# Attention stage of a graph network: one-hots turned in pairs, tile numbers loaded in thirds, source one-hots two tiles ahead

## The chip, the cores and the metric

The kernel runs on one core of a Trainium2 chip. A core has five engines that each work through an instruction stream of their own: PE (matmul), DVE (VectorE), ACT (ScalarE), POOL (GpSimd) and SP, which here mostly starts transfers. They wait for each other by semaphores. The metric is the device time of one execution in microseconds (us).

## The reference, cut to what matters

Two layers of a graph network over 6250 nodes and 206250 edges, sorted by their target node `dst`. The change concerns the first layer, a graph attention with 4 heads of 32 features, which the kernel computes in its attention stage:

```python
h = (x @ W.T).reshape(N, H, OUT)              # x is normalised and clipped first
a_src = (h * att_src).sum(-1)
a_dst = (h * att_dst).sum(-1)
alpha = jax.nn.leaky_relu(a_src[src] + a_dst[dst], 0.2)
amax = jax.ops.segment_max(alpha, dst, num_segments=N)
ex = jnp.exp(alpha - amax[dst])
denom = jax.ops.segment_sum(ex, dst, num_segments=N)
msg = h[src] * (ex / denom[dst])[:, :, None]
out = jax.ops.segment_sum(msg, dst, num_segments=N)
```

The second layer (gathers of node rows, two matmuls for each edge, another sum over targets) follows in stages that the change does not touch.

## The kernel before

**Tiles and batches.** The edges form 1612 tiles of 128, one edge for each partition, and 62 batches (`NB`) of 26 tiles (`BT`). Since the edges are sorted, the targets of a tile lie in two neighbouring tiles of 128 nodes. Their number, the tile's bin, is kept in `bin_row` and is read into engine registers by `bins`: one load of 26 numbers at the start of each batch, on DVE for batch b and on PE for batch b + 2.

**What is done for a tile t of batch b.** POOL gathers the rows h[src] (line 494) into `G`. DVE's `hot` (line 935) writes a one-hot of the targets, 128 edges x 256 nodes in bf16, into `OHb`. PE's `turn` (line 1453) transposes it in two halves into a PSUM bank, one of two; ACT's `turn_out` (line 621) copies it to `ohT`, also two buffers. PE's `expand` (line 1463) multiplies it with the table `aT3` to give each edge the logits of its target. All this is done two batches ahead, for batch b + 2, while batch b is summed. From the logits of batch b + 1 a chain of small steps on DVE, PE and ACT (`chain`, spread over the tiles by `STEPS`) makes the segment maxima and the exponentials; its first step (line 954) also needs the gathered rows of batch b + 1.

For the batch b itself, ACT's `widen` (line 628) copies the one-hot as fp32 into one of four buffers `OH`. DVE's `product` (line 1022) makes the messages `msg`. PE's aggregation (line 1525) multiplies the widened one-hot with the messages into one of two PSUM banks, and DVE's `add_up` (line 1042) adds that bank to the node tile `acc` in SBUF.

**What sets the order.** Each engine's order is written out by hand in its `batch` function, a loop over t; nothing else schedules. In pass t before the change:

- DVE: hot(b+2, t), add_up(b, t-2), then products and a step of the chain.
- PE: turn(b+2, t), expand(b+2, t-1), aggregation(b, t), sometimes small matmuls of the chain.
- ACT: widen(b, t+2), turn_out(b+2, t), sometimes small copies of the chain.

**Who waits for whom.** An aggregation of tile t waits for `acc_done`, that is add_up(t-2) has emptied its bank. add_up(t) waits for `agg_ready` of tile t. widen(t) waits for `agg_ready` of tile t-4, since there are four buffers `OH`. hot(b+2, t) overwrites the slot of tile t in batch b and waits for `wide_ready` of that tile. turn(b+2, t) waits for `oh_ready` of tile t and for `ohT_ready` of tile t-2; turn_out(t) for `ohT_ps` of tile t and for `expanded` of tile t-2. POOL's gather for tile t of batch b+2, where t is odd, waits for `agg_ready` of tile t in batch b.

The first two batches are turned ahead of the loop. Batches 2 to 57 (on ACT to 59) run in hardware loops with two batches in a body, so that a jump comes with every second batch; batches 0, 1 and 58 to 61 are written out.

## Time and profile before

| | us |
|---|---|
| median of 3 runs | 5811.69 |
| lowest, highest run | 5804.10, 5815.06 |
| the profiled execution: time | 5807.29 |
| the profiled execution: span, first to last instruction | 5805.4 |
| attention stage in it | about 149 to 2257 |

| engine | busy us | share of the span |
|---|---|---|
| PE (matmul) | 5114.6 | 88% |
| DVE | 4028.8 | 69% |
| POOL | 3923.5 | 68% |
| ACT | 2891.4 | 50% |

Busy time is the time in which an engine works on an instruction; loads of registers, jumps and waits are not in it. The shares are means over stages that have different limits, so a stage is read by itself. In brackets behind an instruction stands how long its engine sat idle before it and what ended that; "issue" means that the engine waited for nothing that the profile shows.

### The profile page before, as it was taken

Reading aid. Unit: us, or ns where it says so; the run is one execution under the profiler, and the core shown is the slowest. Engines: PE = TensorE matmul, PEld = TensorE weight load, DVE = VectorE, ACT = ScalarE, POOL = GpSimd, SP = SyncE. Lnnn points to the kernel's source line nnn. Section 1 sums busy time; section 2 is a strip of 40 time slices with the busy share of each in tenths; the row PEclk is TensorE's granted clock in tenths of the full one; section 3 lists DMA queues with packets and bytes.
Section 4 is the critical chain, followed back from the end, with each engine's and each line's share of the span. In section 5 each row is a group of like instructions: output and inputs, shape, how many; then the busy total and the mean of one; then the engine's idle time right before and its main releaser. Section 6 shows DMA issues by size and latency. Waiting matters only on the chain.

```text
span 5805.4 us, 160391 instructions
## 1 busy us (share of the span) xinstructions
PE 5114.6 (88%) x34498; PEld 4012.9 (69%) x34499; DVE 4028.8 (69%) x14406; ACT 2891.4 (50%) x8241; POOL 3923.5 (68%) x3713
## 2 busy tenths in 40 slices
PE   4888888888888886899999999999987999999999
PEld 3677777776677775667666666666665777777777
DVE  6777777777777778555555555555555888888887
ACT  3555555555555553333333333333224777777776
POOL 4777777777777775677777777777776545555553
PEclk6898888888888887999999999999998999999999
DMA  4422222222222225899888899988896999999997
GB/s 108 161 54 52 52 53 53 52 53 53 53 52 52 53 62 165 261 262 269 261 263 260 255 262 260 257 261 253 256 256 182 214 214 211 213 216 215 213 214 187
DMA packets 860289, 993.31 MB, mean 171 GB/s; under 512 B 307992, under 2 KB 663224, under 8 KB 859774
## 3 DMA queue, kind: packets, MB, share of 16 engines
q1 hardware_dynamic: 662494, 608.23, 40.1%
q0 software_dynamic: 190592, 378.22, 24.3%
q10 hardware_dynamic: 6816, 3.38, 0.2%
q14 instruction: 349, 2.86, 0.2%
q8 instruction: 38, 0.62, 0.0%
HBM read 726.65 MB, written 262.76 MB: 170 GB/s over the span
## 4 chain that ended last, share of the span: by engine, by line
PE 55%; DMA 12%; DVE 10%; issue 10%; POOL 7%; DVEq 4%; ACT 2%; POOLq 0%; SPq 0%; ACTq 0%
PE bank L1525 12%; PE bank L1684 11%; PE bank L1617 7%; DMA xr<-arena 7%; PE bank L1619 7%; POOL xr L542 7%; PE bank L1674 6%; DMA arena<-p_tab,arena 3%; PE bank L1453 3%; DVE arena L1042 2%; DVEq L246 2%; DVE arena L935 2%; PE bank L1607 1%; DMA arena<-h_tab,arena 1%; PE bank L1665 1%
## 5 line engine op out<-in xcount | busy, mean ns | idle before, releaser
L494 POOL DMA_INDIRECT arena<-h_tab,arena x1612 | 1591.7, 987 | 582.9 <-issue 399.5
L542 POOL DMA_INDIRECT xr<-arena x1612 | 1587.3, 985 | 510.7 <-issue 350.3
L1525 PE MATMUL bank<-arena 128*128 128x136 f32 x6448 | 1299.7, 329 | 96.6 <-DVE arena L1042 8.1
L703 ACT ACTIVATE arena<-bank 128x256 f32<-128x256 f32 x1612 | 595.9, 385 | 1405.6 <-PE bank L1619 1050.2
L556 POOL DMA_INDIRECT arena<-p_tab,arena x428 | 668.4, 1562 | 658.7 <-DMA arena<-p_tab,arena 443.4
L1525 PEld LDWEIGHTS bank<-arena 128*128 128x128 f32 x6448 | 966.3, 211 | 201.8 <-issue 109.0
L621 ACT ACTIVATE arena<-bank 128x256 bf16<-128x256 bf16 x1612 | 618.2, 384 | 888.9 <-PE bank L1453 833.6
L1617 PE MATMUL bank<-arena 128*128 128x256 f32 x3224 | 1010.3, 395 | 42.4 <-DVE arena L1236 25.2
L1619 PE MATMUL bank<-arena 128*128 128x256 f32 x3224 | 972.5, 383 | 28.6 <-DVE arena L1252 25.5
L1684 PE MATMUL bank<-arena 128*128 128x257 f32 x3424 | 898.8, 385 | 3.8 <-ACT arena L780 3.2
L1042 DVE TENSOR_TENSOR arena<-arena,bank 128x272 f32 x1612 | 692.2, 429 | 181.5 <-PE bank L1525 163.7
L1619 PEld LDWEIGHTS bank<-arena 128*128 128x128 f32 x3224 | 605.4, 190 | 148.6 <-DVE arena L1252 69.9
L628 ACT ACTIVATE arena<-arena 128x256 f32<-128x256 bf16 x1612 | 645.1, 408 | 89.7 <-issue 66.7
L1684 PEld LDWEIGHTS bank<-arena 128*128 128x128 f32 x3424 | 586.2, 191 | 75.2 <-issue 5.0
L1617 PEld LDWEIGHTS bank<-arena 128*128 128x128 f32 x3224 | 537.6, 198 | 135.8 <-issue 49.4
L935 DVE TENSOR_SCALAR arena<-arena 128x256 bf16<-128x256 bf16 x1612 | 461.0, 289 | 219.5 <-issue 210.3
L1453 PE MATMUL bank<-arena 128*128 128x128 bf16 x3224 | 489.0, 238 | 136.6 <-DVE arena L935 134.5
L1252 DVE COPY arena<-bank 128x128 f32<-128x128 f32 x806 | 233.2, 289 | 512.4 <-PE bank L1607 512.2
L780 ACT ACTIVATE arena<-arena 128x512 f32<-128x512 f32 x856 | 535.6, 626 | 98.7 <-DVE arena L1347 74.9
L1674 PE MATMUL bank<-arena 128*128 x3852 | 566.8, 274 | 1.9 <-DVE arena L1347 1.0
L1236 DVE TENSOR_SCALAR arena<-arena 128x128 f32<-128x128 bf16 x1612 | 474.1, 306 | 79.9 <-PE bank L1619 46.6
L1347 DVE TENSOR_TENSOR arena<-arena,bank 128x512 f32<-128x512 f32 x856 | 469.0, 548 | 1.8 <-PE bank L1674 1.8
(253 smaller groups left out, 6596.8 us busy)
## 6 DMA issues: line engine op xcount, KB each, us to landing
arena<-xr SPq DMA_DIRECT2D x428, 516.0 KB, 3.9
arena<-q_tab SPq DMA_DIRECT2D x1612, 128.0 KB
arena<-in_edge_attr SPq DMA_DIRECT2D x61, 832.0 KB
arena<-rel_tab SPq DMA_DIRECT2D x124, 224.0 KB
arena<-h_tab,arena POOLq DMA_INDIRECT x1612
xr<-arena POOLq DMA_INDIRECT x1612
arena<-rel_tab SPq DMA_DIRECT2D x124, 192.0 KB
xr<-arena SPq DMA_DIRECT2D x26, 516.0 KB
```

The source lines that it names most:

```text
L494: pool.indirect_dma_start(G[:, q, t, :], None, h_tab, bass.IndirectOffsetOnAxis(ap=idx[:, q, t:t + 1], axis=0)).then_inc(sem(f"gath{q}"), 16)
L542: pool.indirect_dma_start(xr, bass.IndirectOffsetOnAxis(ap=pos[:, q, t:t + 1], axis=0), Rb[:, t, :], None).then_inc(sem(f"scat{m}"), 16)
L556: pool.indirect_dma_start(XR[:, s, k, RW:RW + HID], None, p_tab, bass.IndirectOffsetOnAxis(ap=sidx[:, s, k:k + 1], axis=0), compute_op=ALU ...
L621: A.activation(ohT[:, t % 2, :], PSB[t % 2][:].bitcast(BF16)[:, 0:2 * P], ACT.Copy).then_inc(sem("ohT_ready"), 1)
L628: A.activation(OH[:, (t + 2 * q) % 4, :], OHb[:, q, t, :], ACT.Copy).then_inc(sem("wide_ready"), 1)
L1042: V.tensor_tensor(a, a, PSB[3 + t % 2][:, 0:2 * H * MW], ALU.add).then_inc(sem("acc_done"), 1)
L1453: last = pe.transpose(PSB[t % 2][:].bitcast(BF16)[:, k * P:(k + 1) * P], OHb[:, s, t, k * P:(k + 1) * P], identb)
L1525: last = pe.matmul(PSB[3 + t % 2][:, k * H * MW:(k + 1) * H * MW], OH[:, (t + 2 * q) % 4, k * P:(k + 1) * P], flat(msg[:, t, :, :]), start ...
L1617: pe.matmul(o, OHT[:, (t + 2 * q) % 4, :], Qw[:, t, :], start=True, stop=False)
L1619: pe.matmul(o, EAT[:, (t // 2 + q) % 2, :], w1z[:, t % 2, :], start=False, stop=True).then_inc(sem("main_done"), 1)
L1674: last = pe.matmul(PSB[2 + m % 2][:, j * HID:(j + 1) * HID], ohTp[:, m % 2, j, :], flat(Pt[:, bass.ds(reg, 1), part, :]), start=(part == 0 ...
L1684: last = pe.matmul(PSB[4 + m % 2][:, 0:XW], OHp[:, m, j, :], hid[:, m % 2, j, :], start=(j == 0), stop=(j == PR - 1))
```

## The change

In the batches of the attention stage:

- `turn` and `turn_out` work on a pair g of tiles (2g and 2g+1): four transposes into one PSUM bank, one copy of 512 columns, every second pass. `ohT` has room for two pairs.
- `expand` runs two tiles behind, in pass t for tile t-2; the last two tiles of a batch are expanded in passes 0 and 1 of the next, for which PE reads their two numbers again.
- `hot` runs two tiles ahead: pass t makes tile t+2 of batch b+2, and tiles 0 and 1 of batch b+3 are made at the end of batch b, among the last two add_ups.
- The tile numbers are loaded in three parts of 8 or 9, on DVE in passes 0, 8 and 17, on PE in passes 1, 9 and 18.
- The second half of the logits' sum on DVE moves from pass 1 to pass 3.

The diff, cut to its core:

```diff
         S = Region(Z0)
-        aRes, ohT, OH, msg = S([NT + 1, 2 * H]), S([2, 2 * P], BF16), S([4, 2 * P]), S([BT, H, MW])
+        aRes, ohT, OH, msg = S([NT + 1, 2 * H]), S([2, 2, 2 * P], BF16), S([4, 2 * P]), S([BT, H, MW])
         abS, vE, isl4 = S([2, BT, 2 * H]), S([H, BT]), S([H, BT])
...
             return v.rearrange(f"p {d} -> p ({d})") if len(v.shape) > 2 else v
+        NG2 = BT // 2
+        LOADS = [(k * BT // 3, (k + 1) * BT // 3) for k in range(3)]
         PIECES = [(m * BT // 4, (m + 1) * BT // 4) for m in range(4)]
...
         block = ctx.enter_context(nc.Block())
-        def bins(engine, b, count):
+        def bins(engine, b, lo, count):
             return nc.values_load_multi_w_load_instructions(
-                bin_row[0:1, bass.ds(b * RB, count)], engines=[engine], min_val=0, max_val=NT - 1,
+                bin_row[0:1, bass.ds(b * RB + lo, count)], engines=[engine], min_val=0, max_val=NT - 1,
                 skip_runtime_bounds_check_because="a node's tile, clamped at 0")[1]
...
                     projected(k - 2)
-            def turn_out(b, t, first=False):
-
-                act.wait_ge(sem("ohT_ps"), b * BT + t + 1)
-                if not (first and t < 2):
-                    act.wait_ge(sem("expanded"), b * BT + t - 1)
-                A.activation(ohT[:, t % 2, :], PSB[t % 2][:].bitcast(BF16)[:, 0:2 * P], ACT.Copy).then_inc(sem("ohT_ready"), 1)
+            def turn_out(b, s, g, first=False):
+
+                act.wait_ge(sem("ohT_ps"), b * NG2 + g + 1)
+                if not (first and g < 2):
+                    act.wait_ge(sem("expanded"), b * BT + 2 * g - 2)
+                k = (s * NG2 + g) % 2
+                A.activation(flat(ohT[:, k, :, :]), PSB[k][:].bitcast(BF16)[:, 0:4 * P], ACT.Copy).then_inc(sem("ohT_ready"), 1)
             def widen(b, q, t, first=False):
...
             act.wait_ge(sem("cols_used"), 2)
-            for t in range(BT):
-                turn_out(0, t, True)
+            for g in range(NG2):
+                turn_out(0, 0, g, True)
             act.wait_ge(sem("rb_init"), 2)
...
             chain_exp(0, True)
-            for t in range(BT):
-                turn_out(1, t)
+            for g in range(NG2):
+                turn_out(1, 1, g)
             def batch(b, q, ahead2=True, ahead1=True, first=False):
...
                         widen(b, q, t + 2, first)
-                    if ahead2:
-                        turn_out(b + 2, t)
+                    if ahead2 and t % 2 == 0:
+                        turn_out(b + 2, q, t // 2)
                     if ahead1 and t == 1:
...
                 b, n = 2 * i + q, 2 * i + q + 1
-                regs = bins(ENG.DVE, b, BT)
+                regs = []
                 for t in range(BT):
-                    if ahead2:
-                        hot(b + 2, q, t)
+                    if ahead2 and t + 2 < BT:
+                        hot(b + 2, q, t + 2)
+                    for lo, hi in LOADS:
+                        if t == lo:
+                            regs += bins(ENG.DVE, b, lo, hi - lo)
                     if t == 0:
...
                         V.tensor_tensor(a, a, fac.unsqueeze(2).to_broadcast([P, H, MW]), ALU.mult).then_inc(sem("acc_done"), 1)
-                        if ahead1:
-                            logits(b + 1, 1 - q, 1)
                     if t >= 2:
                         add_up(b, t - 2, regs)
+                    if ahead1 and t == 3:
+                        logits(b + 1, 1 - q, 1)
                     if t in (3, 7):
...
                         product(1 - q, 1, 3)
-                add_up(b, BT - 2, regs)
-                add_up(b, BT - 1, regs)
+                for t in range(2):
+                    if ahead3:
+                        hot(b + 3, 1 - q, t)
+                    add_up(b, BT - 2 + t, regs)
                 if table == "runs":
...
             logits(1, 1, 0)
+            for t in range(2):
+                hot(2, 0, t)
             batch(0, 0)
...
                 last.then_inc(sem("counted"), 1)
-            def turn(b, s, t, first=False):
-                pe.wait_ge(sem("oh_ready"), b * BT + t + 1)
-                if not (first and t < 2):
-                    pe.wait_ge(sem("ohT_ready"), b * BT + t - 1)
-                for k in range(2):
-                    last = pe.transpose(PSB[t % 2][:].bitcast(BF16)[:, k * P:(k + 1) * P], OHb[:, s, t, k * P:(k + 1) * P], identb)
+            def turn(b, s, g, first=False):
+                u = (s * NG2 + g) % 2
+                pe.wait_ge(sem("oh_ready"), b * BT + 2 * g + 2)
+                if not (first and g < 2):
+                    pe.wait_ge(sem("ohT_ready"), b * NG2 + g - 1)
+                for t in range(2):
+                    for k in range(2):
+                        last = pe.transpose(PSB[u][:].bitcast(BF16)[:, (2 * t + k) * P:(2 * t + k + 1) * P], OHb[:, s, 2 * g + t, k * P:(k + 1) * P], identb)
                 last.then_inc(sem("ohT_ps"), 1)
-            def expand(b, t, regs, first=False):
-
-                pe.wait_ge(sem("ohT_ready"), b * BT + t + 1)
+            def expand(b, s, t, reg, first=False):
+
+                g = t // 2
+                if t % 2 == 0:
+                    pe.wait_ge(sem("ohT_ready"), b * NG2 + g + 1)
                 half, j = divmod(t, BT // 2)
...
                 for k in range(2):
-                    last = pe.matmul(ab_ps[half][:, j, :, :].rearrange("p s c -> p (s c)"), ohT[:, t % 2, k * P:(k + 1) * P],
-                                     flat(aT3[:, bass.ds(regs[t] + k, 1), :, :]), start=(k == 0), stop=(k == 1))
+                    last = pe.matmul(ab_ps[half][:, j, :, :].rearrange("p s c -> p (s c)"), ohT[:, (s * NG2 + g) % 2, t % 2, k * P:(k + 1) * P],
+                                     flat(aT3[:, bass.ds(reg + k, 1), :, :]), start=(k == 0), stop=(k == 1))
                 last.then_inc(sem("expanded"), 1)
...
             pe.wait_ge(sem("hx_used"), NCH)
-            regs = bins(ENG.PE, 0, BT)
-            for t in range(BT):
-                turn(0, 0, t, True)
-                if t:
-                    expand(0, t - 1, regs, True)
-            expand(0, BT - 1, regs, True)
+            regs = bins(ENG.PE, 0, 0, BT)
+            for g in range(NG2):
+                turn(0, 0, g, True)
+                for t in range(max(2 * g - 2, 0), 2 * g):
+                    expand(0, 0, t, regs[t], True)
+            for t in range(BT - 2, BT):
+                expand(0, 0, t, regs[t], True)
             chain_resets(0)
...
             chain_carry(0)
-            regs = bins(ENG.PE, 1, BT)
-            for t in range(BT):
-                turn(1, 1, t)
-                if t:
-                    expand(1, t - 1, regs)
-            expand(1, BT - 1, regs)
+            regs = bins(ENG.PE, 1, 0, BT - 2)
+            for g in range(NG2):
+                turn(1, 1, g)
+                for t in range(max(2 * g - 2, 0), 2 * g):
+                    expand(1, 1, t, regs[t])
             def batch(b, q, ahead2=True, ahead1=True, first=False, table=""):
-                if ahead2:
-                    regs = bins(ENG.PE, b + 2, BT)
+                regs, late = [], bins(ENG.PE, b + 1, BT - 2, 2) if ahead1 else []
                 pe.wait_ge(sem("g_ready"), b + 1)
...
                 for t in range(BT):
+                    if ahead2 and t % 2 == 0:
+                        turn(b + 2, q, t // 2)
+                    if t < 2 and ahead1:
+                        expand(b + 1, 1 - q, BT - 2 + t, late[t])
                     if ahead2:
-                        turn(b + 2, q, t)
-                        if t:
-                            expand(b + 2, t - 1, regs)
+                        for lo, hi in LOADS:
+                            if t == lo + 1:
+                                regs += bins(ENG.PE, b + 2, lo, hi - lo)
+                        if t >= 2:
+                            expand(b + 2, q, t - 2, regs[t - 2])
                     pe.wait_ge(sem("wide_ready"), b * BT + t + 1)
...
                                 step(b + 1)
-                if ahead2:
-                    expand(b + 2, BT - 1, regs)
             batch(0, 0, first=True)
...
```

Where instructions stand now. First ACT, around passes 2 and 3 of a batch in the loop; the 256-column copy from a PSUM bank is `turn_out`, the 128x256 copy within `arena` (the SBUF) is `widen`, the copies 1x4x26 to 1x4 are the chain's resets. Before:

```order
L627 REGISTER_ALU [waits agg_ready]
L628 ACTIVATE arena<-arena 128x256 [waits oh_ready]
L618 REGISTER_ALU
L621 ACTIVATE arena<-bank 128x256 [waits expanded,ohT_ps]
```

After:

```order
L620 REGISTER_ALU
L624 ACTIVATE arena<-bank 128x512 [waits expanded,ohT_ps]
L639 ISA [waits cin_ready]
L639 ACTIVATE arena<-arena 1x4x26
L640 ISA
L640 ACTIVATE arena<-arena 1x4x25
L641 ACTIVATE arena<-arena 1x4
L630 REGISTER_ALU [waits agg_ready]
L631 ACTIVATE arena<-arena 128x256 [waits oh_ready]
```

Before, each widen was followed by one copy from PSUM; now one copy of twice the width stands ahead of two widens.

Next PE, passes 4 and 5 of a batch in the loop: `turn` (128x128), `expand` (128x24), aggregation (128x136), and a transpose of the chain (104x128). Before, for one pass:

```order
L1449 REGISTER_ALU
L1453 MATMUL bank<-arena 128x128 [waits ohT_ready,oh_ready]
L1453 MATMUL bank<-arena 128x128
L1463 ISA [waits ohT_ready]
L1463 MATMUL bank<-arena 128x24
L1463 ISA
L1463 MATMUL bank<-arena 128x24
L1518 REGISTER_ALU
L1521 REGISTER_ALU [waits msg_ready,wide_ready]
L1525 MATMUL bank<-arena 128x136 [waits acc_done]
L1525 MATMUL bank<-arena 128x136
```

After, for the even pass (the odd one has no turn and its `expand` no wait):

```order
L1460 REGISTER_ALU
L1465 MATMUL bank<-arena 128x128 [waits ohT_ready,oh_ready]
L1465 MATMUL bank<-arena 128x128 x3
L1472 REGISTER_ALU
L1477 ISA [waits ohT_ready]
L1477 MATMUL bank<-arena 128x24
L1477 ISA
L1477 MATMUL bank<-arena 128x24
L1537 REGISTER_ALU
L1540 REGISTER_ALU [waits msg_ready,wide_ready]
L1544 MATMUL bank<-arena 128x136 [waits acc_done]
L1544 MATMUL bank<-arena 128x136
```

All four transposes of a pair stand behind the aggregation of the odd tile before it.

Last DVE, at the first instructions of the loop's body: `hot` is the TENSOR_SCALAR 128x256, the tile numbers the TENSOR_LOAD. Before:

```order
L1147 ISA
L246 TENSOR_LOAD arena
L934 ISA
L935 ISA [waits wide_ready]
L935 TENSOR_SCALAR arena<-arena 128x256
L1052 REGISTER_ALU
L1053 TENSOR_SCALAR arena<-bank 128x4 [waits fac_ps]
```

After:

```order
L1157 ISA
L938 ISA [waits wide_ready]
L938 TENSOR_SCALAR arena<-arena 128x256
L248 ISA
L248 TENSOR_LOAD arena
L1058 REGISTER_ALU
L1059 TENSOR_SCALAR arena<-bank 128x4 [waits fac_ps]
```

The load is now behind the first `hot` and is a third as long; the `hot` is that of tile 2.

## Rows read from the trace of the kernel before

**Rows 1.** Windows, attention stage: length, busy time (instructions) by engine, PEclk, DMA share, GB/s.

```profile
149.00:2257.00 2108.00, 1736.97 (x14171) 1483.63 (x14171) 1658.67 (x6311) 1164.01 (x3599) 1534.80 (x1569) 0.88 0.26 65
```

**Rows 2.** Groups by line, 500 to 1800 us: busy us, mean ns, idle before.

```profile
L494 POOL DMA_INDIRECT arena<-h_tab,arena x986 | 967.6, 981 | 333.6 <-issue 242.1 <-PE bank L1525 91.5
...
L628 ACT ACTIVATE arena<-arena 128x256 f32<-128x256 bf16 x984 | 393.5, 407 | 45.2 <-issue 45.1
L621 ACT ACTIVATE arena<-bank 128x256 bf16<-128x256 bf16 x983 | 377.1, 384 | 535.4 <-PE bank L1453 500.9 <-PE bank L1463 14.9 <-issue 12.5
```

**Rows 3.** Waits, 500 to 1800 us: total us, times, longest.

```profile
POOL arena L494 <- PE bank L1525: 91.5, 235, 2.7
...
DVE arena L954 <- DMA arena<-h_tab,arena: 24.2, 19, 1.9
```

**Rows 4.** Timeline around two starts of a batch: start, duration, [idle before <-releaser].

```profile
1037.36 0.95 POOL L494 DMA_INDIRECT arena<-h_tab,arena  x1 [0.30 <-issue]
1037.99 1.03 ACT L628 ACTIVATE arena<-arena 128x256 f32<-128x256 bf16 x3 [2.48 <-issue]
...
1041.69 0.43 DVE L935 TENSOR_SCALAR arena<-arena 128x256 bf16<-128x256 bf16 x1 [4.92 <-issue]
...
1073.60 0.29 DVE L935 TENSOR_SCALAR arena<-arena 128x256 bf16<-128x256 bf16 x1 [1.99 <-issue]
```

**Rows 5.** Timeline, one tile at full clock, same columns.

```profile
1048.40 0.43 DVE L1042 TENSOR_TENSOR arena<-arena,bank 128x272 f32 x1
...
1049.11 0.53 PEld L1525 LDWEIGHTS bank<-arena 128*128 128x128 f32 x4 [0.21 <-DVE arena L1042]
...
1050.00 0.72 PE L1525 MATMUL bank<-arena 128*128 128x136 f32 x4
...
1050.45 0.21 PEld L1453 LDWEIGHTS bank<-arena 128*128 128x128 bf16 x2
...
1050.56 0.28 PE L1453 MATMUL bank<-arena 128*128 128x128 bf16 x2
...
1050.87 0.38 ACT L621 ACTIVATE arena<-bank 128x256 bf16<-128x256 bf16 x1 [0.20 <-PE bank L1453]
...
1051.15 0.41 ACT L628 ACTIVATE arena<-arena 128x256 f32<-128x256 bf16 x1
1051.33 0.26 DVE L935 TENSOR_SCALAR arena<-arena 128x256 bf16<-128x256 bf16 x1
...
1051.51 0.43 DVE L1042 TENSOR_TENSOR arena<-arena,bank 128x272 f32 x1
```

**Rows 6.** Timeline, batches 59 and 60: who waits for ACT, ACT for PE.

```profile
2135.79 1.03 ACT L628 ACTIVATE arena<-arena 128x256 f32<-128x256 bf16 x3 [2.67 <-issue]
2136.28 0.29 DVE L935 TENSOR_SCALAR arena<-arena 128x256 bf16<-128x256 bf16 x1 [1.89 <-ACT arena L628]
...
2220.85 0.42 ACT L628 ACTIVATE arena<-arena 128x256 f32<-128x256 bf16 x1 [0.56 <-PE bank L1525]
```

**Rows 7.** Source lines, tile-number loads, 26 (L246) and 12 (L252): ns min/median/max.

```profile
L246 DVEq TENSOR_LOAD <-arena x62: 2060/2070/4694, 141.5 to 2233.8; - x62
...
L252 DVEq TENSOR_LOAD <-arena x108: 845/852/1094, 4439.0 to 5760.0; - x108
```

**Rows 8.** Source line, an ACT copy of 512 columns in a later stage.

```profile
L780 ACT ACTIVATE arena<-arena x65: 618/625/634, 4599.7 to 4698.7; 128x512 f32<-128x512 f32 x65
```

**Rows 9.** Windows, after a start, in mid-batch, in a last batch.

```profile
1042.00:1048.00 6.00, 5.75 (x36) 5.43 (x36) 4.47 (x18) 3.54 (x13) 3.79 (x5) 0.53 0.21 48
1049.00:1070.00 21.00, 19.61 (x180) 16.58 (x180) 20.26 (x81) 13.40 (x41) 15.36 (x16) 1.00 0.21 47
2216.00:2233.00 17.00, 14.90 (x98) 11.63 (x97) 15.51 (x57) 8.61 (x22) 0.00 (x0) 0.93 0.41 107
```

**Rows 10.** Timeline, PE's weight loads at half clock.

```profile
1043.85 0.96 PEld L1525 LDWEIGHTS bank<-arena 128*128 128x128 f32 x4
...
1044.70 0.38 PEld L1453 LDWEIGHTS bank<-arena 128*128 128x128 bf16 x2
```

## The prediction

> **What bounds the kernel now.** I read the stages first. The attention stage runs from about 149 to 2257 us; every other stage issues the same instructions in both kernels. Over it PE, DVE and POOL are all 73% to 82% busy, so no share names the bound [rows 1]. The groups by line say more: 986 gathers (L494) keep POOL for 967.6 us with 333.6 us idle ahead of them, one every 1.32 us, so a batch of 26 takes 34.3 us [rows 2]. An unhindered gather takes 0.95 us with 0.30 us ahead of it [rows 4], 1.25 in all, 32.6 us for a batch. POOL is therefore nearly the bound, and in every second batch DVE waits for gathered rows [rows 3]. PE and DVE are close behind: DVE stands idle for 2.0 us where a batch starts inside the loop body and for 4.9 us where the loop closes, every second batch [rows 4].
>
> The last view is one tile at full clock [rows 5]. PE's aggregation of tile t (L1525) needs add_up(t - 2) on DVE (L1042); one aggregation starts 0.89 us after the other (1049.11 and 1050.00). ACT's two copies are only used a tile or more later, so nothing waits for them. That slack is what the change spends.
>
> **The change part by part.** *Removed.* The 26 tile numbers are one load of 2.07 us on DVE [rows 7], and PE's is alike. It explains the stall of 2.0 us inside the body, and 2.07 of the 4.9 us at the loop's end; the other 2.8 us is the jump. 12 numbers take 0.85 us [rows 7], so one costs (2.07 - 0.85) / 14 = 0.087 us and a third, 8 or 9 numbers, an estimated 0.6 to 0.75 us. The bounds are nothing, where the engine waits anyway, and 0.85, the load of 12. The Trainium skill ("DMA: Bandwidth & Descriptors", Latency and other measured facts) gives such a load a floor of about 600 ns. No row here has fewer than 12 numbers to show it; by it PE's new load of two numbers would cost 0.6 instead of 0.17 us, some 25 us more over 60 batches.
>
> *Turned in pairs.* PE turns two one-hots in a row, and ACT copies 512 columns instead of twice 256. The copy of 256 holds ACT for 0.28 us, from 1050.87 to 1051.15 [rows 5]. A further 256 columns cost 0.625 - 0.408 = 0.22 us by ACT's other copies [rows 2, 8], or 0.28 if all is doubled. The pair holds ACT for 0.50 to 0.56 us; I take 0.53. [...]
>
> *One-hots two tiles ahead.* This part decides. On DVE hot(b+2, t+2) now stands ahead of add_up(t - 2), and it waits for wide_ready of tile t + 2: ACT must first have widened the old one-hot of that slot. widen(t + 2) in turn waits until aggregation t - 2 has freed one of four buffers. Before, DVE asked here for widen(t), which needed aggregation t - 4. Two tiles of slack are gone. Queued behind that wait on DVE is add_up(t - 2), and for that PE's aggregation t waits. ACT's order makes it worse: for even t it runs widen(t + 2), the paired copy, widen(t + 3), and the copy waits for PE's turn, which PE issues behind aggregation t - 1. So there is a ring: aggregation t - 1, turn, paired copy, widen(t + 3), hot(t + 3), add_up(t - 1), aggregation t + 1. Its steps at full clock:
> - from the aggregation's start to the turn behind it, 1050.00 to 1050.56: 0.56 us [rows 5]
> - the turn until ACT starts, 1050.56 to 1050.87: 0.31, and 0.21 for two more transposes by their weight loads: 0.52 [rows 5]
> - the paired copy, until widen can start: 0.53
> - widen 0.41, and 0.07 to the hot that waited for it (the first of three widens that start at 2135.79 ends at 2136.20; hot starts at 2136.28): 0.48 [rows 2, 6]
> - from hot to add_up's start, 1051.33 to 1051.51: 0.18 [rows 5]
> - from add_up's start to the aggregation that waited for it, 1048.40 to 1049.11: 0.71 [rows 5].
>
> That is 2.98 us for two tiles, above the 1.8 they take in these rows and above the 2.5 that two gathers take. Bounds: 2.88 with the copy at 0.50 and no hand-over; 3.22 with the copy at twice 0.384. At half clock the aggregation's weights take 0.96 instead of 0.53 us and a turn's 0.38 instead of 0.21 [rows 10], so the ring takes 0.43 + 0.34 more, some 3.8. That a widen can wait for an aggregation and start at its end is seen in the last batches, where ACT has nothing else to do [rows 6].
>
> *The sum for a batch.* The ring binds from tile 1 to tile 23, 11 turns: 32.8 us. Once in each batch there also lie on it: ACT's three small copies and DVE's logits around tiles 2 to 4, about 0.7; PE's small matmuls behind aggregation 7, which wait for the backward scan and so start late, about 0.9; the one behind aggregation 11, 0.5; and the load on DVE at tile 17, between hot and add_up, 0.7. That makes 2.8, an estimate whose parts are sums of operations of 0.2 to 0.4 us; its bounds are 1.4 and 4. The loads on DVE at tiles 0 and 8 fall where it waits over 1 us for ACT, and PE's ahead of aggregations that wait for add_up: nothing there, 0.7 each without that cover. Tiles 23 to 25 take twice 0.9 to 1, as now: 1.9. From tile 25 to tile 1 of the next batch PE issues a small matmul, the first pair, two late expansions, an aggregation and its load, about 3.3. Inside the body a batch takes 32.8 + 2.8 + 1.9 + 3.3 = 40.8 us.
>
> At the loop's end hot(b+3, 0) on DVE waits for widen(b+1, 0), which ACT does only after its own jump of 2.5 us [rows 4]; the last add_ups and DVE's jump of 2.8 come behind that. The two jumps lay side by side, now one follows the other: about 4 us above a start inside the body, 44.8. Both batches: 85.6. After each start PE's clock is low for some us (0.53 from 1042 to 1048, full from 1049) [rows 9]; one ring and a third at 3.8 instead of 2.98 adds 1.1 a batch: 87.8.
>
> Against 2 x 34.3 = 68.6 now that is 19.2 us more for two batches. 60 of the 62 batches turn one-hots ahead: 30 x 19.2 = 576 us. The two batches turned before the loop get some 3 us quicker (0 to 6). The profiled execution took 5807.29 us, 1.9 above its span and 4.4 under the median of the runs, 5811.69. 5807 + 576 - 3 = 6380, and halfway to the median's basis **6383 us**.
>
> **The rivals.** *A: the gathers stay the bound, and it gets faster.* If the ring closes in less than the 2.5 us of two gathers, only the gain at the starts counts. PE holds POOL up for 91.5 us in 235 cases [rows 3], of which 235 x 0.30 = 70.5 is POOL's usual gap: 21 us in 37.9 batches, 0.55 each, and 60 of them vanish: -33, and -2 at the tail: 5772. For it speaks that DVE already waits for gathered rows in every second batch, so that POOL needs only a little more speed elsewhere; against it, that the ring would have to lose 0.5 us, one whole step.
>
> *B: parity.* The ring takes just 2.5 to 2.6 us and what the starts give back covers it: 5800 to 5820. It asks for a coincidence.
>
> *C: the clock stays low.* In the ring PE waits about 1 us in three. In the last batches, where it waits some 0.4 us a tile, it kept 0.93 of the clock [rows 9]. If these gaps hold it at 1.2 GHz, the ring is 3.8 and PE's side work doubles: 9 us for the ring and about 3.6 for the rest, so 53.4 and 57.4 us, 110.8 for two batches, 5807 + 30 x 42.2 = 7070. The last batches are the nearer row.
>
> That the change doesn't do what it says is excluded: ACT's order has the copy of 512 columns, DVE's the three loads.
>
> **How the numbers follow.** The ring 0.85, A 0.07, B 0.03, C 0.05. The ring's own range: 11 x 0.10 for its cheapest steps, 1.1 for no slow stretch and 1.4 for half the side work are 3.6 us a batch, 60 x 3.6 = 216 less, 6167; 11 x 0.24 and another 1.1 of slow stretch are 3.7, 222 more, 6605. A, B and C stay outside with 0.15: 6165 to 6610. Slower by over 0.2%, about what a measurement of this kernel can tell from no change: 0.90; within it 0.03; faster 0.07.
>
> **What would show it.** Right: the attention stage is some 570 us longer and nothing else is; DVE's hot waits mostly for ACT's widen, the paired copy for PE's turn; aggregations start about 1.2 and 1.8 us apart in turn; DVE no longer waits for gathered rows, and POOL waits for PE some 7 us a batch or more; the loads take 0.6 to 0.75 us. Wrong: aggregations at a steady 1.25 us and DVE waiting for gathers in every batch (A), or a granted clock near 0.5 throughout (C). Most open is the ring's length: 0.1 us in it is 66 us in the time.

## The result and the profile after

The changed kernel takes 6863.67 us (median of four runs, 6856.78 to 6866.68) against 5810.42 (5804.1 to 5815.06): 1.181 times as long, 95% interval 1.179 to 1.183. The direction was forecast, the size was not: 573 us were expected, 1053 came, and 6863.67 lies above the range's end of 6610.

The profiled execution's span is 6854.9 us, 1049.5 above that of before. Sections 1 and 2 of its page, with each row of 40 slices of 171 us:

```profile
span 6854.9 us, 157771 instructions
...
PE 5753.4 (84%) x34498; PEld 4607.2 (67%) x34499; DVE 4091.6 (60%) x14406; ACT 2829.3 (41%) x7435; POOL 3876.6 (57%) x3713
...
PE   5777777777777777777699999999999799999999
...
POOL 4444444444444444445477777777777745555553
PEclk6555555555556555656899999999999999999999
```

The first 19 slices are the attention stage. POOL is busy 0.4 of them where it was 0.7 of [rows 1], and the granted clock (PEclk) is 0.5 to 0.6 of full speed throughout. The first and the last gather start at 76.8 and 3262.0 us, before at 76.8 and 2208.4: this stage is 1053.6 us longer and everything behind it is as before.

The windows (columns as in [rows 1]: length, busy time of PE, PEld, DVE, ACT, POOL, then PEclk): the whole stage, 36 us in the middle, and one of the few stretches at full clock.

```profile
1512.00:1548.00 36.00, 27.87 (x147) 24.13 (x148) 19.02 (x70) 11.16 (x28) 15.61 (x16) 0.50 0.13 30
...
1560.00:1572.00 12.00, 7.63 (x66) 6.07 (x63) 8.83 (x32) 5.66 (x16) 7.81 (x9) 1.00 0.20 46
155.00:3300.00 3145.00, 2361.79 (x14064) 2056.22 (x14064) 1712.39 (x6278) 1095.30 (x2792) 1489.54 (x1561) 0.57 0.18 43
```

0.57 stands where [rows 1] has 0.88. The groups by line over 600 to 2800 us answer [rows 2] (busy us, mean ns, idle time before):

```profile
L496 POOL DMA_INDIRECT arena<-h_tab,arena x1098 | 1049.0, 955 | 1154.1 <-PE bank L1544 899.5 <-issue 254.6
...
L624 ACT ACTIVATE arena<-bank 128x512 bf16<-128x512 bf16 x549 | 327.8, 597 | 1278.5 <-PE bank L1477 960.2 <-PE bank L1465 318.3
...
L938 DVE TENSOR_SCALAR arena<-arena 128x256 bf16<-128x256 bf16 x1097 | 320.2, 292 | 815.9 <-ACT arena L631 799.1 <-issue 15.0
...
L957 DVE TENSOR_TENSOR arena<-arena 128x104 f32<-128x104 f32 x42 | 14.2, 339 | 0.0
```

A gather (L496) is as fast as before, but 1098 in 2200 us are 2.0 us for each, 52.1 for a batch, and POOL waits 899.5 us for PE. DVE's hot (L938) waits 799.1 us for ACT's widen (L631); in before it waited for widen once after the first batches, for 1.9 us [rows 6]; L957, which waited for gathered rows in every second batch [rows 3], has no idle time at all in this stretch. So the gathers no longer set the pace. The waits, same stretch (total, times, longest), show who does:

```profile
ACT arena L624 <- PE bank L1477: 960.2, 462, 3.3
...
DVE arena L938 <- ACT arena L631: 799.1, 568, 3.1
PEld bank L1544 <- DVE arena L1045: 445.7, 501, 3.0
```

PE waits for DVE's add_up (L1045), DVE for ACT, ACT for PE: a ring. (The first line names the expansion, L1477, which PE issues behind the turn. But the copy's own wait is for an expansion one pass earlier, done before the turn starts; ends on PE are modelled, and what the copy waits for is the turn, L1465.) One turn of it in the timeline (start, duration, [idle before <-releaser]), which answers [rows 5]:

```profile
1512.01 1.27 PE L1544 MATMUL bank<-arena 128*128 128x136 f32 x4 [0.49 <-DVE arena L1045]
...
1513.07 0.63 PE L1465 MATMUL bank<-arena 128*128 128x128 bf16 x4
...
1513.50 0.25 PE L1477 MATMUL bank<-arena 128*128 x2
...
1513.60 1.25 PE L1544 MATMUL bank<-arena 128*128 128x136 f32 x4
...
1513.82 0.60 ACT L624 ACTIVATE arena<-bank 128x512 bf16<-128x512 bf16 x1 [1.74 <-PE bank L1477]
...
1514.32 0.41 ACT L631 ACTIVATE arena<-arena 128x256 f32<-128x256 bf16 x1
...
1514.87 0.51 DVE L938 TENSOR_SCALAR arena<-arena 128x256 bf16<-128x256 bf16 x1 [0.37 <-ACT arena L631]
...
1515.12 0.44 DVE L1045 TENSOR_TENSOR arena<-arena,bank 128x272 f32 x1
...
1515.61 1.28 PE L1544 MATMUL bank<-arena 128*128 128x136 f32 x4 [0.50 <-DVE arena L1045]
```

Aggregation to turn 1.06, turn to paired copy 0.75, copy to widen 0.50, widen to hot 0.55, hot to add_up 0.25, add_up to aggregation 0.49: 3.60 us for two tiles, each step in the order that the prediction gave. This is the ring at half clock (an aggregation holds PE for 1.27 us; at full clock for 0.73). Elsewhere in mid-batch the steps from aggregation to aggregation are 2.0 and 1.6 us in turn as well. The chain of work that ended last (start, duration, what) runs round the same ring:

```profile
1532.27 1.27 PE bank L1544 x4
1533.54 0.44 PE bank L1465 x4
...
1534.58 0.42 ACT arena L631
...
1535.38 0.45 DVE arena L1045
```

### The profile page after: what moved, and what is told of

Same layout as the page of the kernel before. It is cut to its first block, busy times and chain, and to the rows that moved or that the text cites. A ratio compares the mean times of both kernels' runs of the same rounds, so it can differ in the third digit from the quotient of the medians.

```text
span 6854.9 us, 157771 instructions
## 1 busy us (share of the span) xinstructions
PE 5753.4 (84%) x34498; PEld 4607.2 (67%) x34499; DVE 4091.6 (60%) x14406; ACT 2829.3 (41%) x7435; POOL 3876.6 (57%) x3713
## 4 chain that ended last, share of the span: by engine, by line
PE 56%; issue 12%; DVE 8%; DMA 8%; ACT 6%; POOL 5%; DVEq 4%; ACTq 0%; POOLq 0%; SPq 0%
PE bank L1544 16%; PE bank L1701 10%; DMA xr<-arena 6%; PE bank L1634 6%; PE bank L1691 6%; PE bank L1636 6%; POOL xr L544 5%; PE bank L1465 4%; DVE arena L1045 4%; ACT arena L631 3%; DVEq L248 2%; PE bank L1624 1%; PE bank L1682 1%; ACT arena L624 1%; DVE arena L938 1%
## 5 line engine op out<-in xcount | busy, mean ns | idle before, releaser
L496 POOL DMA_INDIRECT arena<-h_tab,arena x1612 | 1551.3, 962 | 1676.8 <-PE bank L1544 1257.5
L1544 PE MATMUL bank<-arena 128*128 128x136 f32 x6448 | 1856.7, 440 | 597.8 <-DVE arena L1045 572.8
L1544 PEld LDWEIGHTS bank<-arena 128*128 128x128 f32 x6448 | 1416.8, 300 | 684.8 <-DVE arena L1045 593.6
L624 ACT ACTIVATE arena<-bank 128x512 bf16<-128x512 bf16 x806 | 480.9, 597 | 1842.5 <-PE bank L1477 1318.8
L938 DVE TENSOR_SCALAR arena<-arena 128x256 bf16<-128x256 bf16 x1612 | 467.8, 293 | 1149.0 <-ACT arena L631 1130.8
L558 POOL DMA_INDIRECT arena<-p_tab,arena x428 | 667.7, 1560 | 659.9 <-DMA arena<-p_tab,arena 453.2
L1634 PE MATMUL bank<-arena 128*128 128x256 f32 x3224 | 1011.3, 396 | 33.6 <-DVE arena L1246 19.2
L1045 DVE TENSOR_TENSOR arena<-arena,bank 128x272 f32 x1612 | 696.7, 432 | 197.5 <-issue 155.6
L631 ACT ACTIVATE arena<-arena 128x256 f32<-128x256 bf16 x1612 | 649.1, 411 | 201.3 <-PE bank L1544 194.1
L1636 PEld LDWEIGHTS bank<-arena 128*128 128x128 f32 x3224 | 607.1, 191 | 149.5 <-DVE arena L1262 71.4
L1701 PEld LDWEIGHTS bank<-arena 128*128 128x128 f32 x3424 | 586.0, 191 | 74.5 <-issue 6.0
L1634 PEld LDWEIGHTS bank<-arena 128*128 128x128 f32 x3224 | 539.6, 198 | 125.3 <-issue 42.9
L1465 PE MATMUL bank<-arena 128*128 128x128 bf16 x3224 | 474.0, 297 | 137.8 <-DVE arena L938 136.7
L1465 PEld LDWEIGHTS bank<-arena 128*128 128x128 bf16 x3224 | 363.4, 139 | 216.3 <-DVE arena L938 145.0
```

Source lines behind the costliest of these rows:

```text
L496: pool.indirect_dma_start(G[:, q, t, :], None, h_tab, bass.IndirectOffsetOnAxis(ap=idx[:, q, t:t + 1], axis=0)).then_inc(sem(f"gath{q}"), 16)
L558: pool.indirect_dma_start(XR[:, s, k, RW:RW + HID], None, p_tab, bass.IndirectOffsetOnAxis(ap=sidx[:, s, k:k + 1], axis=0), compute_op=ALU ...
L631: A.activation(OH[:, (t + 2 * q) % 4, :], OHb[:, q, t, :], ACT.Copy).then_inc(sem("wide_ready"), 1)
L1045: V.tensor_tensor(a, a, PSB[3 + t % 2][:, 0:2 * H * MW], ALU.add).then_inc(sem("acc_done"), 1)
L1465: last = pe.transpose(PSB[u][:].bitcast(BF16)[:, (2 * t + k) * P:(2 * t + k + 1) * P], OHb[:, s, 2 * g + t, k * P:(k + 1) * P], identb)
L1544: last = pe.matmul(PSB[3 + t % 2][:, k * H * MW:(k + 1) * H * MW], OH[:, (t + 2 * q) % 4, k * P:(k + 1) * P], flat(msg[:, t, :, :]), start ...
```

## Experiments

The runs came in groups, each on one chip. In the first comparison and in one group before takes 5810 and 5818 us, in the four other groups, on four chips, 7264 to 7390, so ratios are compared only within a group or between chips of the same kind. Behind each ratio stands what before takes on its chip; the long kind is described last, with r0_before. Ranges in us in the expectations were written for a chip where before takes 5810 us, and e1 to e6, i1 to i3, j1 and j2 all fell on the long kind, where the changed kernel loses 3% (r1_changed) and not 18%. Of the openings of the ring only both together (h3_both_aligned) were run on the first kind.

**Does hot ahead of add_up close the ring?** The first, **e1_hot_behind**, changes only the order of these two on DVE (and likewise in the batch's last two passes):

```diff
-                    if ahead2 and t + 2 < BT:
-                        hot(b + 2, q, t + 2)
                     ...
                     if t >= 2:
                         add_up(b, t - 2, regs)
+                    if ahead2 and t + 2 < BT:
+                        hot(b + 2, q, t + 2)
```

> The changed kernel, with one order on DVE swapped: hot(b+2, t+2) stands behind add_up(t-2), and at the end of a batch each hot(b+3, ..) behind its add_up. Theory (a ring runs from an aggregation over the turn, the paired copy, widen, hot and add_up to the next aggregation): DVE no longer waits for ACT ahead of add_up, the ring then spans four tiles instead of two, aggregations come about 1.1 to 1.3 us apart and PE's granted clock in the stage is back above 0.8; time 5750 to 6050 us, with the loop's end as the open part. Rival (the pairs themselves, or the loads in thirds, make the stage slow): the swap changes little, above 6700 us.

Measured, before 7390 us: 0.985 (0.982 to 0.988). The same kernel once more as **i2_hot_behind**, on another chip of that kind (before 7264):

> The changed kernel with one thing put back in spirit: hot(b+2, t+2) stands behind add_up(t - 2) on DVE instead of ahead of it, so that a late widen no longer holds add_up. Pairs, thirds and the load of 9 from place 17 stay. Theory (hot ahead of add_up closes the ring, and the rest of the change costs little): 1.00 to 1.03 of before, granted clock over 0.8. Rival (pairs themselves, or the loads, are what costs): over 1.1.

0.985 (0.983 to 0.988) again, where the changed kernel takes 1.031 (r1_changed, on another chip of the long kind; on i2's own chip i4_sizes, the changed kernel with some 25 us of extra work, took 1.037 in one run). The granted clock over 800 to 1800 us is 0.71 and 0.73 where r1_changed has 0.58, not the 0.8 expected, though before has only 0.70 on such a chip. Pairs, thirds and the load at place 17 are all still there; moving one instruction behind another takes away more than the whole loss on this kind of chip.

**e2_copy_odd** opens the ring at another place: the paired copy stands in odd passes, behind widen(t + 2) of an odd t.

```diff
-                    if ahead2 and t % 2 == 0:
+                    if ahead2 and t % 2 == 1:
                         turn_out(b + 2, q, t // 2)
```

> The changed kernel, with one order on ACT changed: the paired copy is made in odd passes, behind widen(t+3), instead of in even passes ahead of it. hot stays ahead of add_up. Theory: the turn and the copy leave the ring; what is left is aggregation, widen, hot, add_up, aggregation, about 0.73 + 0.04 + 0.48 + 0.18 + 0.71 = 2.1 to 2.4 us for two tiles at full clock, under the 2.5 of two gathers; 5800 to 6100 us. Rival (it is the wait for one of the four widened buffers alone that makes DVE wait): still there unchanged, about 6860 us.

1.010 (1.007 to 1.013): some two thirds of the loss go, hot's wait for widen is 209.2 us in 1000 and PE's for add_up is still there. **e5_both** has both edits:

> The changed kernel with both rings opened: hot(b+2, t+2) behind add_up(t-2) on DVE, and the paired copy in odd passes behind widen(t+3) on ACT. Theory: no ring under 2.5 us for two tiles is left, the gathers are the bound again and PE no longer holds POOL up at the loop's end: 5770 to 5830 us, 0.99 to 1.00 of before, clock above 0.85. Rival (pairs and late expansions cost by themselves): 6000 or more.

0.983 (0.980 to 0.986, before 7362), hardly more than e1 alone gives. Its clock over 800 to 1800 us is 0.69, not the 0.85 expected.

**Which part makes the ring?** **e3_hot_alone** is the kernel before with nothing but hot two tiles ahead, ahead of add_up; **e4_hot_back** is the changed kernel with `hot(b + 2, q, t)` as in before, so with pairs and thirds but without the two tiles.

> The kernel before with only the one-hots moved two tiles ahead on DVE; turns, copies and expansions tile by tile, tile numbers in one load. Theory: the same ring with half the turn and half the copy, 0.56 + 0.31 + 0.28 + 0.48 + 0.18 + 0.71 = 2.52 us for two tiles at full clock, about 3.1 at half clock: 5950 to 6500 us, DVE's hot waiting for ACT's widen. Rival (the pairs are the cause): 5811 us as before, or less.

> The changed kernel without the one-hots two ahead: hot(b+2, t) in pass t as before, with pairs, late expansions and loads in thirds kept. Theory: the ring over widen is gone, but turn(g) on PE now needs hot(2g+1), which stands on DVE behind add_up(2g-2) and the products of that pass: aggregation 2g-2, add_up, products, hot, turn, aggregation 2g, 2.4 to 3 us for two tiles: 6000 to 6600 us. If the one-hots ahead were the whole cause: 5780 to 5820 us. If they were none of it: 6860 us.

1.0155 (1.0125 to 1.0185) and 1.030 (1.027 to 1.034), before 7390. The waits of each over 800 to 1800 us say what the ratios can't. e3_hot_alone:

```profile
DVE arena L935 <- ACT arena L628: 282.8, 253, 5.6
```

e4_hot_back:

```profile
DVE arena L1045 <- PE bank L1540: 317.7, 286, 3.5
PE bank L1461 <- DVE arena L938: 179.2, 107, 6.3
```

With single turns hot waits for widen already, 253 times in 20 batches, and in this stretch of before not once, on either kind of chip: the ring is there without the pairs. Pairs without hots ahead are as slow as the whole change, for another reason: PE's pair needs the hot of tile t + 1, which DVE makes only in the next pass, so PE waits for hot and add_up for PE. The change's parts need each other: pairs need hots ahead, and hots ahead need to stand behind add_up.

**What is the low clock worth?** **r1_changed** is the changed kernel, **e6_fill** the same with four matmuls that nobody reads in the gap of every second tile:

```diff
                             expand(b + 2, q, t - 2, regs[t - 2])
+                        if t % 2 == 1:
+                            for k in range(4):
+                                pe.matmul(PSB[1 - (q * NG2 + t // 2) % 2][:, 0:2 * P], identb, iotab, start=True, stop=True)
```

> The changed kernel once more on the chip of this group, as the base for the next two. If the chip is like the first one: 6860 us, 1.18 of before, clock near 0.57 in the attention stage.

> The changed kernel with four matmuls more in each odd pass on PE (bf16, 256 columns, into the PSUM bank that no other engine reads then), ahead of the aggregation that waits for add_up; their result is not used. They cost 4 x 0.21 = 0.85 us at half clock and 0.43 at full clock, in a place where PE waits 0.7 us and 1.1 us. Theory (the ring's waits hold PE at 1.2 GHz, and the clock is why the ring takes 3.6 instead of 3.0 us): with the gap filled the granted clock in the stage rises from 0.57 to over 0.85 and the time falls, although PE has more to do, from 6860 to 6300 to 6550 us. Rival (the clock is not tied to these gaps): clock stays near 0.57, time 6860 to 7000.

1.031 (1.029 to 1.034) and 1.015 (1.012 to 1.017), before 7362: with more to do on PE the kernel is 123 us faster. **i1_fill** and **j1_fill** are e6_fill again, both on chips of the long kind (before 7264 and 7270), and gave 1.018 (1.015 to 1.021) and 1.019 (1.018 to 1.021).

> The changed kernel in which PE also runs four matmuls of 256 columns that nobody reads in every second tile, where it would wait for add_up. On a chip where the changed kernel takes 1.18 of before. Theory (the gaps of the ring hold PE's clock low, and that lengthens the ring's steps): the granted clock over 800 to 1800 us rises from 0.54 to over 0.8, and the time falls, though PE has more to do: the ring goes from 3.6 towards 3.0 us, 11 x 0.6 = 6.6 us a batch, less about 1 for the extra matmuls, so some 300 us, to about 1.13 of before. Rival (the clock is low for another reason, or costs little): within 0.5% of the changed kernel, or slower. On a chip where before takes about 7370 us it would be the 1.015 seen there.

The window of i1_fill and its aggregations at tiles in mid-batch:

```profile
800.00:1800.00 1000.00, 708.87 (x5680) 571.03 (x5679) 567.55 (x2059) 353.15 (x919) 495.93 (x520) 0.86 0.15 36
```

```profile
1439.96 0.73 PE L1547 MATMUL bank<-arena 128*128 128x136 f32 x4 [1.17 <-DVE arena L1045]
...
1442.72 0.71 PE L1547 MATMUL bank<-arena 128*128 128x136 f32 x4
...
1444.73 0.73 PE L1547 MATMUL bank<-arena 128*128 128x136 f32 x4 [0.81 <-DVE arena L1045]
...
1445.62 0.61 PE L1547 MATMUL bank<-arena 128*128 128x136 f32 x3
```

The clock goes from 0.58 in r1_changed to 0.86 (0.85 in e6_fill, on r1_changed's own chip), and this turn of the ring takes 2.90 us instead of 3.6 (1442.72 to 1445.62), beside the 2.98 forecast for full clock. That PE's idle time in the ring holds the clock down, and that the clock goes into its length, is thereby shown. At which point it switches is not: in the changed kernel 12 us with PE busy 7.63 have full clock (1560 to 1572 above), and 36 us with 27.87 have half. Nor is the whole price shown: 491 gathers in 1000 us are 53.0 us a batch, 519 in e6_fill are 50.1, so the clock is worth at least 2.9 us a batch net of the added matmuls, where 5.6 were expected. The added work lengthens some turns (the median of two steps is 3.4), and on a chip where before takes 5810 this kernel was never run.

**The load that is too long.** In after, [rows 7] has this answer (source line, min/median/max ns):

```profile
L248 DVEq TENSOR_LOAD <-arena x186: 602/853/4935, 146.2 to 3301.6; - x186
```

Taken one by one the three loads of a batch take 0.60, 0.85 and 2.07 us on DVE, in each of the eight batches looked at, though the last two both load nine numbers; PE's take 0.59, 0.85 and 2.18. In the chain of work (start, duration) and in the timeline the third is the longest stop of a batch behind its start:

```profile
1538.85 2.07 DVEq L248
1541.18 0.45 DVE arena L1045
```

```profile
1541.67 1.27 PE L1544 MATMUL bank<-arena 128*128 128x136 f32 x4 [2.90 <-DVE arena L1045]
```

**h2_aligned** only cuts the thirds elsewhere; **h1_changed** is its base.

```diff
-        LOADS = [(k * BT // 3, (k + 1) * BT // 3) for k in range(3)]
+        LOADS = [(0, 8), (8, 16), (16, BT)]
```

> The changed kernel once more, as the base of this group: about 1.03 of before if the chip is like the last one (before near 7370 us), about 1.18 if it is like the first (before near 5810 us).

> The changed kernel with the thirds cut at 0, 8 and 16 instead of 0, 8 and 17, so that the last load begins at a number whose place in its row is a multiple of 4. In the trace after, the load of 9 numbers from place 8 takes 0.85 us and the load of 9 from place 17 takes 2.07 us on DVE and 2.18 on PE, in every batch, though both load 9. Theory (a load's time goes by where it starts, not only by how many numbers it takes): the last load, now 10 numbers from place 16, takes about 0.85 us on both queues, the steps at tiles 16 to 18, 4.2 and 3.3 us in the changed kernel, fall by some 2.5 us together, and the time by 60 x 2.5 = 150 us, to about 0.98 of the changed kernel. Rival (it is the third load's place in the program, or something that runs beside it): the load still takes 2.07 us and the time stays where it is, within 0.3%.

Before 5818 us: h1_changed 6874.83, 1.182 (1.180 to 1.184); h2_aligned 6722.49, 1.155 (1.153 to 1.157), 152 us less. **i4_sizes** measures the loads by themselves (two tiny copies behind each use its numbers; in h4_sizes, where nobody uses them, the trace has none of the extra loads and the time is the changed kernel's, 6874.41 us):

> The changed kernel with fourteen extra loads on DVE, and two tiny copies behind each that use their numbers, ahead of the first batch; an earlier kernel for this had loads whose numbers nobody used, and they were not issued at all. Row of batch 1, whose start is a multiple of 4 numbers: 2, 4, 8, 9, 12 and 26 numbers from place 0, 9 from 8, 10 from 16, 9 from 17, 4 from 17, 9 from 1, 9 from 2, 9 from 4, 25 from 1. Theory (a start off a multiple of 4 makes it slow): 0.55, 0.55, 0.60, 0.85, 0.85, 2.07; 0.85, 0.85; then 2.07 and less for 4; slow again from 1 and perhaps 2, 0.85 from 4; 25 from 1 over 2.07, up to 6 us if each number goes by itself at 0.23 us. Rival (by count alone): 9 numbers take the same from every place.

The timeline shows the copies; the idle time before each, put down to "issue", is the load and 0.02 us. In order: 4, 9 and 26 numbers from place 0, 10 from 16, 9 from 17, 4 from 17, 25 from 1. Left out are 8 from place 0 with 0.61 us, 12 from 0, 9 from 8 and 9 from 4 with 0.87 each, 9 from 1 and 9 from 2 with 2.08 each, and 2 from 0, whose idle time isn't its load alone.

```profile
169.16 0.27 DVE L1159 COPY arena<-arena 1x1 int32 x2 [0.38 <-issue]
...
171.19 0.27 DVE L1159 COPY arena<-arena 1x1 int32 x2 [0.89 <-issue]
...
174.70 0.27 DVE L1159 COPY arena<-arena 1x1 int32 x2 [2.11 <-issue]
...
177.19 0.27 DVE L1159 COPY arena<-arena 1x1 int32 x2 [1.09 <-issue]
179.55 0.27 DVE L1159 COPY arena<-arena 1x1 int32 x2 [2.09 <-issue]
180.80 0.27 DVE L1159 COPY arena<-arena 1x1 int32 x2 [0.98 <-issue]
...
192.51 0.27 DVE L1159 COPY arena<-arena 1x1 int32 x2 [5.60 <-issue]
```

The times fit a rule: from a place that is a multiple of four, four numbers go together and a rest goes one by one; from any other place every number goes by itself. The trace shows times, not accesses. Counted so (4: 1 access, 8: 2, 9: 3, 12: 3, 10: 4, 26: 8; unaligned 4: 4, 9: 9, 25: 25), a load takes an estimated 0.14 us and 0.20 to 0.25 for each access. The rival by count alone falls.

**How much is left with ring and load mended?** **h3_both_aligned** is e5_both with the cuts at 0, 8 and 16.

> Both openings of the ring (hot behind add_up, the paired copy in odd passes) and the loads cut at 0, 8 and 16. With the ring open the load at tile 17 holds DVE where it has some slack: the theory expects 1 to 2.5 us less a batch than with both openings alone, which took 0.983 of before on one of the chips: 0.965 to 0.975 of before. If the gathers or the clock set the pace there, nothing: 0.98.

5837.40 us, 1.0035 (1.0025 to 1.0045) of before's 5818, above what was expected; it differs from h2_aligned by the two orders alone, and that is 885 us. So the loss of 1057 us in this group comes apart: 152 for where the third load starts, 885 for the two orders, and 20 that stay. Its window answers that of after:

```profile
800.00:1800.00 1000.00, 811.05 (x6712) 706.42 (x6711) 800.80 (x2976) 537.47 (x1330) 725.38 (x752) 0.85 0.23 52
```

The clock is back at 0.85, beside before's 0.87 in the same stretch, and 752 gathers are 34.6 us a batch, beside 34.2. From 1400 to 1540 us its batches take 34.4, 31.7, 34.3 and 37.0 us at clocks of 0.90, 1.00, 0.91 and 0.77. The dearest has the lowest clock; that the clock is why the gain at the starts is lost was not tested.

**The part that can gain, alone.** **i3_before_thirds** is the kernel before with loads cut at 0, 8 and 16 and nothing else, **j2_before_thirds** the same with more rounds.

> The kernel before with the tile numbers loaded in three pieces, cut at 0, 8 and 16 so that each starts at a multiple of 4, and nothing else: each piece 0.6 to 0.85 us. The stall of 2.0 us where a batch starts inside the body, and 2.07 of the 4.9 at the loop's end, go; the loads at tiles 8 and 16 come where DVE has at most some tenths of a microsecond to spare. If the gathers set the pace between the starts, up to 1.4 us less a batch is possible and 0.3 is likely: 0.98 to 1.00 of before. Rival (DVE is nearly the bound, and two loads more in each batch cost it what the start gives back): 1.00 to 1.01.

> The kernel before with the tile numbers loaded in three pieces cut at 0, 8 and 16, and nothing else, once more. Where before takes about 7300 us: 0.995 again. Where it takes about 5810: POOL's gathers are nearer to the bound there, 1.25 of 1.32 us for each, so the 2 us that DVE gains at each start can give at most (1.32 - 1.25) x 26 = 1.8 us a batch, and I expect 0.3 to 1: 0.990 to 0.997. Rival (two loads more in each batch cost DVE what the start gives back): 1.00 to 1.01.

0.995 (0.993 to 0.997) and 0.994 (0.9925 to 0.996), before 7264 and 7270: a small gain, real there. For a chip where before takes 5810 it is not known.

**What differs on the other chips.** **r0_before** is the kernel before on one of them.

> The kernel before once more, for a profile on the chip of this group: all kernels of the group are compared with it. On the chip of the first four experiments it took 7390 us where it took 5810 before, and engines there stood still for 1 to 3 us at places where nothing holds them. Both theories expect 5810 us and gathers 1.32 us apart on a chip without that, and 7390 with it.

7378.81 us. Its gathers run from 75.5 to 3087.1 us, so the attention stage alone takes 880 us more than on the first chip, while the changed kernel's (76.3 to 3333.0) takes only 72 more; the stages behind it take 690 and 660 us more in both. The timeline shows stops for which no instruction accounts; the profile gives "remote" as what ended some of them:

```profile
1003.63 0.73 PE L1525 MATMUL bank<-arena 128*128 128x136 f32 x4
...
1005.69 0.38 ACT L621 ACTIVATE arena<-bank 128x256 bf16<-128x256 bf16 x1 [2.37 <-remote]
1005.83 0.44 DVE L1042 TENSOR_TENSOR arena<-arena,bank 128x272 f32 x1 [2.43 <-PE bank L1525]
```

PE's aggregation ends at 1004.36, DVE starts on it 1.5 us later. Over 800 to 1800 us 131 waits end so in r0_before, 130 in e5_both and 118 in i3_before_thirds, some 6 a batch, 19 in r1_changed, and none in before, after and h3_both_aligned on the first kind of chip. So the changed kernel hardly has them, and its ring takes the same 3.6 us as on the first chip. Why that is so, and what the stops are, is open. The change costs 3% there and 18% here because before's attention stage is slower there, not because the changed kernel's is faster.

## Why the prediction was right in direction and wrong in size

**What bounds.** Right. The bound moved from the gathers to the ring, with the order of steps and the hand-overs that the prediction gave, and the two orders are 885 of the 1057 us.

**The ring's length.** Right at both levels: 2.98 forecast and 2.90 seen at full clock (i1_fill), 3.8 forecast and 3.60 seen at half. The paired copy is 0.60 us busy and holds the next step for 0.50; 0.53 was taken.

**The clock.** This is the step that failed. The prediction took full clock except for 1.1 us a batch, since the last batches, the "nearer row", kept 0.93 with gaps of some 0.4 us a tile [rows 9], and gave the low clock throughout (rival C) 0.05. In the ring PE waits about 0.7 us in every second tile (the 0.71 ahead of its aggregations). The granted clock was 0.50 over 1512 to 1548 and 0.57 over the stage. That was rival C's mechanism, at a smaller price than its 7070 us: C put 0.82 us on every turn of the ring (9 us a batch) and 3.6 on the rest, and the trace shows 0.62 a turn, for some 0.86 of the time. In the row of the last batches PE was busy 14.90 of 17 us, and its waits for add_up there are 0.27 to 0.37 us long, against 27.87 of 36 us and 0.71 in the ring; the row did not resemble the ring at the one point that counted, and the chance did not reflect that.

**The load at tile 17.** Also wrong. From 26 numbers in 2.07 and 12 in 0.85 us [rows 7] the prediction drew a straight line, 0.087 us a number, and took 0.7 us for a third. By the rule above the time goes by accesses, 8 against 3, and nine numbers from place 17 are nine accesses: 2.07 us. PE's third load is as long (2.18 us) and was put at nothing; it lies on the path too, the step from tile 17 to 18 is 3.2 to 3.3 us instead of 1.6. Mending the start alone gave 152 us. PE's load of two numbers takes 0.55 us (the shortest of L248 on PE's queue is 544 ns), not the 0.17 of the straight line. The Trainium skill ("DMA: Bandwidth & Descriptors", Latency and other measured facts) gives such a load a floor of about 600 ns; the trace is near it for the two-number load, and below it for four numbers in i4_sizes, 0.38 us.

**The loop's end.** Right in size, by luck; the mechanism was another. 4 us above a start inside the body were forecast. From tile 25 to tile 1 of the next batch PE takes 3.3 us either way in most batches (3.3 forecast), and then:

```profile
1504.07 1.25 PE L1544 MATMUL bank<-arena 128*128 128x136 f32 x4
...
1505.57 0.28 DVE L938 TENSOR_SCALAR arena<-arena 128x256 bf16<-128x256 bf16 x1 [2.90 <-ACT arena L631]
...
1509.98 1.27 PE L1544 MATMUL bank<-arena 128*128 128x136 f32 x4 [0.27 <-DVE arena L1045]
```

5.9 us from tile 1 to 2, and 5.4 to 6.2 at the other loop ends from 600 to 1700 us, where a start inside the body has 1.1 to 1.8. The prediction had ACT's jump first and DVE's behind it. But ACT jumps while its last copy still runs (its branch is at 1499.9), and its three widens start without a wait; in before they had one of 2.48 us [rows 4]:

```profile
1500.31 1.05 ACT L631 ACTIVATE arena<-arena 128x256 f32<-128x256 bf16 x3
```

The chain of work shows two stops on DVE instead:

```profile
1502.39 2.92 issue
...
1505.57 0.28 DVE arena L938
1505.85 1.79 issue
1507.75 0.61 DVEq L248
```

The first is DVE's jump (branch at 1502.3), with the hot at 1505.57 right behind it; the profile names widen, which had ended at 1504.72. The second lies between this hot and the load and comes at every loop end looked at; its cause is open. With the load DVE stands idle for 5.5 us, where before lost 4.92 [rows 4]: at the loop's end the shorter load gained nothing.

**The sum.** 1053 us are 35.1 for two batches; 19.2 were forecast, 15.9 are missing. The load's start is 152 / 30 = 5.1 of it, measured. For the other 10.8 the clock suffices: 22 turns of the ring at 3.60 instead of 2.98 are 13.6 us, tiles 23 to 25 at 2.75 instead of 1.9 another 1.7; a mean of 0.57 between the levels 0.5 and 1 means 0.86 of the time at half clock, so 0.86 x 15.3 = 13.2, less the 2.2 that the prediction had for slow clock: 11.0. This last term is worked out from the rows, not isolated by a run; the runs show 2.9 us a batch of it, on other chips. The side work, forecast as 2.1 us a batch beside the load, came to 2.2 by offsetting errors: nothing at tiles 2 to 4, and 1.1 each behind aggregations 7 and 11, where 0.9 and 0.5 stood.

**The rivals.** A and B fell: the gathers are idle half the time. A's condition, a ring that loses a step, is what e1_hot_behind and e5_both make true, and even then h3_both_aligned comes out 0.35% above before on the first kind of chip, where the starts were to give 35 us.

## What to carry to other kernels

Before an instruction is moved earlier on an in-order engine, write down the oldest event that it waits for, and follow what stands behind it round to that event: if the circle closes, its length is the new pace. If it leaves gaps on PE, price the circle at half clock as well, and let the clock's chance be large unless a row with gaps of the same size and rhythm speaks against it. Cut register loads at multiples of four numbers, and with work done ahead put it behind the instruction that others wait for.

## What the runs showed of the hardware

A register load's time goes by where it starts: nine numbers took 0.85 us from a multiple of four and 2.07 from elsewhere, and 25 took 5.58; twelve and nine numbers from place 0 took the same on DVE. PE's clock stood at 0.50 over 36 us in which PE was busy for 27.87, and added work that nobody reads brought it from 0.58 to 0.85 on one chip and made the kernel 123 us faster. Behind its jump at a loop's end DVE stood still for 2.9 us, and for 1.8 more behind its first instruction. And one and the same program took 5810 to 5818 us in two groups and 7264 to 7390 us on four other chips, with stops of 1 to 2 us at hand-overs that a tighter order of work suffers more from than a slack one.
